# Two equal lists for a routed mixture: the order of row and weight loads changed, and context products moved to the next opening

## What is computed

```python
def _L2_ffn_ref(x, router_logits, gating_einsum, linear, per_expert_scale, router_scale):
...
    var = jnp.mean(jnp.square(x.astype(jnp.float32)), axis=-1, keepdims=True)
    router_input = x * jax.lax.rsqrt(var + 1e-06).astype(dtype)
    root_size = jax.lax.rsqrt(jnp.array(F, dtype=dtype))
    router_input = router_input * root_size * router_scale.astype(dtype)
    logits = jnp.einsum('gsd,de->gse', router_input, router_logits.astype(dtype))
    logits32 = logits.astype(jnp.float32)
    probs = jax.nn.softmax(logits32, axis=-1)
    _, choices = jax.lax.approx_max_k(logits32, k=k)
    indicator = jax.nn.one_hot(choices, E, dtype=probs.dtype).sum(axis=-2)
    renorm = jnp.sum(indicator * probs, axis=-1, keepdims=True)
    renorm = jnp.where(renorm > 0.0, renorm, 1.0)
    weights = probs / renorm
    x_flat = x.reshape((-1, F))
    batch_size = G * S
    choices_flat = choices.ravel()
    xs_order = choices_flat.argsort()
    xs_reverse_argsort = xs_order.argsort()
    xs_indices = jnp.repeat(jnp.arange(batch_size), k)[xs_order]
    sorted_xs = x_flat[xs_indices, :]
    choices_oh = jax.nn.one_hot(choices, num_classes=E, dtype=jnp.int32)
    tokens_per_expert = jnp.sum(choices_oh, axis=(0, 1, 2))
    combine_weights = (choices_oh.astype(jnp.float32) * jnp.expand_dims(weights, axis=2)).sum(axis=-1).astype(weights.dtype)
    w_gate = jnp.transpose(gating_einsum, (0, 3, 1, 2)).reshape(E, F, 2 * H)
    gate_out = jax.lax.ragged_dot(sorted_xs, w_gate.astype(dtype), group_sizes=tokens_per_expert)
    gate_out = gate_out.reshape(gate_out.shape[0], 2, H)
    activation = jax.nn.gelu(gate_out[:, 0, :]) * gate_out[:, 1, :]
    expert_outputs = jax.lax.ragged_dot(activation, linear.astype(dtype), group_sizes=tokens_per_expert)
    expert_indices = jnp.repeat(jnp.arange(E), tokens_per_expert, total_repeat_length=expert_outputs.shape[0])
    expert_outputs = expert_outputs * per_expert_scale.astype(expert_outputs.dtype)[expert_indices, None]
    out = expert_outputs[xs_reverse_argsort].reshape((G, S, k, -1))
    out = jnp.einsum('blkd,blk->bld', out, combine_weights, preferred_element_type=out.dtype)
    return out
```

```python
    kvx = jnp.einsum('bsi,oi->bso', cond, w_kv_x)
    kx, vx = jnp.split(kvx, 2, axis=-1)
    kx = _ln(kx.reshape(b, sc, g, d), kxln_w, kxln_b)
    vx = vx.reshape(b, sc, g, d)
    xout = _gqa(qx, kx, vx).reshape(b, s, nh * d)
```

## Time and profile before

| | us |
|---|---|
| median of three runs | 1403.51 |
| lowest, highest | 1401.1, 1404.28 |
| profiled execution | 1401.32 |
| its span, first to last instruction | 1399.6 |

### The profile page before, as it was taken

The page is one execution under the profiler, slowest core; times in us unless marked ns, Lnnn a source line. Parts: engine busy times, 40 slices in busy tenths (PEclk is TensorE's granted clock), DMA queues, the critical chain, the costliest instruction groups (busy, mean ns, idle before and its releaser), DMA issues.

```text
span 1399.6 us, 23540 instructions
## 1 busy us (share of the span) xinstructions
PE 1272.7 (91%) x7122; PEld 1067.1 (76%) x7122; DVE 965.6 (69%) x2457; ACT 814.7 (58%) x2055; POOL 671.1 (48%) x720
## 2 busy tenths in 40 slices
PE   6999999997899999978559789999999999999994
PEld 3556888885688888868558478888887788888884
DVE  7997556766877777543226577878777787877753
ACT  6954222334666766634224486677777778776353
POOL 1112555542444444442124266666768767675444
PEclk9999999999999999989779999999999999999997
DMA  6224555452212232245234693000240001024283
GB/s 237 83 91 134 171 168 165 114 175 80 101 62 91 81 99 94 101 167 186 90 126 144 230 335 120 1 2 1 64 140 31 31 32 61 31 59 162 85 302 115
DMA packets 90140, 159.62 MB, mean 114 GB/s; under 512 B 9325, under 2 KB 50953, under 8 KB 89516
## 3 DMA queue, kind: packets, MB, share of 16 engines
q1 hardware_dynamic: 82811, 144.55, 31.4%
q0 software_dynamic: 6640, 12.67, 2.7%
q10 hardware_dynamic: 576, 1.05, 0.2%
HBM read 103.86 MB, written 58.17 MB: 116 GB/s over the span
## 4 chain that ended last, share of the span: by engine, by line
PE 69%; DVE 12%; issue 6%; ACT 4%; DMA 4%; POOL 4%; SPq 0%; ACTq 0%; POOLq 0%; DVEq 0%
PE ps L1609 9%; PE ps L1741 9%; PE ps L1714 8%; PE ps L1692 7%; PE ps L1759 7%; PE ps L1623 5%; PE ps L1881 5%; PE ps L1724 5%; PE ps L1703 3%; PE ps L1442 3%; DMA mid_x<-mid_rows 2%; POOL urs L1147 2%; PE ps L1892 2%; DVE usum L3242 1%; PE ps L2046 1%
## 5 line engine op out<-in xcount | busy, mean ns | idle before, releaser
L1154 POOL TENSOR_TENSOR probs<-probs,prec 128x512 f32<-128x512 f32 x192 | 202.7, 1056 | 280.5 <-DVE prec L3278 280.5
L2463 ACT ACTIVATE probs<-ps,nmax 128x256 f32<-128x256 f32 x384 | 179.3, 474 | 184.8 <-DVE nmax L3271 119.0
L1714 PE MATMUL ps<-k_feat,q_feat 128*128 128x256 f32 x768 | 198.6, 381 | 2.7 <-ACT q_feat L2453 1.9
L1741 PE MATMUL ps<-probs_t,v_tok 128*128 128x256 f32 x768 | 197.7, 380 | 0.2 <-ACT ob L2482 0.2
L1147 POOL TENSOR_TENSOR urs<-uve,neg_half 128x4 f32<-128x4 f32 x136 | 137.2, 1009 | 52.2 <-DVE uve L3243 41.5
L1714 PEld LDWEIGHTS ps<-k_feat,q_feat 128*128 128x128 f32 x768 | 136.7, 191 | 16.6 <-issue 3.5
L1741 PEld LDWEIGHTS ps<-probs_t,v_tok 128*128 128x128 f32 x768 | 130.9, 190 | 10.4 <-issue 0.6
L1724 PE MATMUL ps<-ident,probs 128*128 128x128 f32 x768 | 116.4, 274 | 14.9 <-ACT probs_t L2472 13.4
L1724 PEld LDWEIGHTS ps<-ident,probs 128*128 128x128 f32 x768 | 92.4, 141 | 48.0 <-issue 20.9
L2472 ACT ACTIVATE probs_t<-ps 128x512 f32<-128x512 f32 x192 | 115.8, 603 | 2.7 <-PE ps L1724 2.7
L2382 ACT ACTIVATE gated<-ps 128x512 f32<-128x512 f32 x48 | 28.8, 599 | 135.5 <-PE ps L1609 135.5
(11 more groups left out here) (489 smaller groups left out, 3437.1 us busy)
## 6 DMA issues: line engine op xcount, KB each, us to landing
rows_in<-zero_rows SPq DMA_DIRECT2D x3, 5200.0 KB, 33.9
mid_more_w<-in_l2f_w SPq DMA_DIRECT2D x14, 768.0 KB, 4.3
tile_w<-in_l3f_w SPq DMA_DIRECT2D x21, 385.5 KB, 6.7
mid_rows<-mid_zero SPq DMA_DIRECT2D x6, 1040.0 KB, 5.6
w<-in_l1f_w SPq DMA_DIRECT2D x24, 256.0 KB, 4.9
spread_w<-we_dram SPq DMA_DIRECT2D x16, 384.0 KB, 3.7
mid_w<-in_l2f_w SPq DMA_DIRECT2D x8, 768.0 KB, 5.9
kv_cross<-kv_out SPq DMA_DIRECT2D x20, 256.0 KB, 2.0
```

The lines of the kernel that those rows point to most:

```text
L1154: pool.tensor_tensor(p3, p3, spread(prec[g % 3][:, :], [P, TB, S]), ALU.mult)\
L1714: mm = pe.matmul(ps[g % 2][:, j * S:(j + 1) * S], q_feat[:, h, j * P:(j + 1) * P], k_feat[:, kv, :], start=True, stop=True)
L1741: mm = pe.matmul(ps[6][:, 0:S], v_tok[:, tb, kv * P:(kv + 1) * P], probs_t[g % 2][:, tb, :], start=tb == 0, stop=tb == TB - 1)
L2463: ins = act_e.activation(probs[g % 4][:, j, :], ps[g % 2][:, j * S:(j + 1) * S], ACT.Exp, bias=nmax[g % 3][:, j:j + 1], **kw, accum_out=ps ...
```

## The change

Two lists of two batches each take the place of lists of three and one. Both have 8 fixed and 7 later tiles: list A is tiles 0 to 14, list B tiles 15 to 29. Only batches 0 and 1 are routed ahead of the loop; batches 2 and 3 are routed inside it, each with steps of its own. SP's order is written anew: rows are issued in runs, and the weight sets behind them. The three context products ahead of the first tile move into the opening of the next attention, and all eight late products are stored behind the loads of `mid_got` and of `wo` (the next attention's output weights). The next norm of batch 2 moves from the end of the loop into the opening, and the turns of batches 0 and 1 to loop turns 26 and 27.

```diff
-KV_LATE_AT = ((-6, -4, -3), (-7, -5, -4))
+KV_LATE_AT = ((-6, -4, -3), (-6, -5, -5, -4, -4, -3))
...
-MID_TILES = ((0, 19), (19, 30))
-MID_LATER = (11, 3)
-MID_BLOCKS = (6, 2)
-MID_BASE = (0, 6 * MID + 1)
-MID_LISTS = 6 * MID + 1 + 2 * MID + 1
+MID_TILES = ((0, 15), (15, 30))
+MID_LATER = (7, 7)
+MID_BLOCKS = (4, 4)
+MID_BASE = (0, 4 * MID + 1)
+MID_LISTS = 2 * (4 * MID + 1)
...
-KV_WITH_MID = 3
...
-                sp.wait_ge(*mid_at("placed", 16 * CHOICES * 3 * TB))
+                half = NT // 2
+                sp.wait_ge(*mid_at("placed", 16 * CHOICES * half))
+                sp.wait_ge(s["o_ready"], L2X.total)
                 for j in range(MID_RING):
                     rows(j)
                 experts_of, blocks = registers(0)
                 sp.wait_ge(s["out_ready"], L2X.total)
                 for i in range(MID_SETS):
                     later(i)
-                store_kv(len(KV_ALL) - KV_GAPS[2], len(KV_ALL) - KV_GAPS[2] + KV_WITH_MID, kv_late)
                 first_b = MID_TILES[1][0]
                 for j in range(MID_RING, first_b):
                     rows(j)
-                    i = j - MID_RING - 3 + MID_SETS
-                    if MID_SETS <= i < MID_LATER[0]:
-                        later(i)
+                later(MID_SETS)
+                later(MID_SETS + 1)
                 sp.wait_ge(*mid_at("placed", 16 * CHOICES * NT))
-                for j in range(first_b, first_b + MID):
+                for j in range(first_b, first_b + 4):
                     rows(j)
+                later(MID_SETS + 2)
+                rows(first_b + 4)
                 more = registers(1)
                 experts_of, blocks = experts_of + more[0], blocks + more[1]
-                for i in range(MID_LATER[0], sum(MID_LATER)):
+                for i in range(4):
+                    later(MID_SETS + 3 + i)
+                    rows(first_b + 5 + i)
+                for j in range(first_b + 9, MID_ALL - 3):
+                    rows(j)
+                for i in range(4):
+                    sp.wait_ge(*mid_put_all(first_b, i))
+                for b in range(2):
+                    load_mid_got(b)
+                for j in range(MID_ALL - 3, MID_ALL):
+                    rows(j)
+                for i in range(sum(MID_LATER) - 3, sum(MID_LATER)):
                     later(i)
                 for i in range(4):
-                    sp.wait_ge(*mid_put_all(first_b, i))
-                kv_all_stored(len(KV_ALL) - KV_GAPS[2] + KV_WITH_MID)
-                for b in range(3):
+                    sp.wait_ge(*mid_put_all(MID_ALL, i))
+                for b in range(2, B):
                     load_mid_got(b)
-                for j in range(first_b + MID, MID_ALL):
-                    rows(j)
-                store_kv(len(KV_ALL) - KV_GAPS[2] + KV_WITH_MID, len(KV_ALL) - 3, kv_late)
-                for i in range(4):
-                    sp.wait_ge(*mid_put_all(MID_ALL, i))
-                load_mid_got(3)
...
-            store_kv(len(KV_ALL) - 3, len(KV_ALL), kv_late)
+            store_kv(len(KV_ALL) - KV_GAPS[2], len(KV_ALL), kv_late)
...
-                if t == 65:
+                if t == 63:
                     pool.wait_ge(*mid_at("zeroed", 16 * MID_ZERO_AT))
                     pool.wait_ge(*mid_at("places", 1))
-                if 65 <= t < 69:
+                if 63 <= t < 67:
                     mid_scatter(2)
 
             run(attention(L2X, beside_l2x))
-            pool.wait_ge(*mid_at("places", 2))
-            mid_scatter(4)
             part_scales(1)
             root_mean_square(2)
             for j in range(MID_ALL):
                 pool.indirect_dma_start(mid_out[:, :], bass.IndirectOffsetOnAxis(ap=mid_to[:, j:j + 1], axis=0),
                                         mid_y[j % 4][:, :], None, bounds_check=CHOICES * NTOK - 1,
                                         oob_is_err=False).then_inc(mid_signal(f"put{j % 4}"), 16)
-                if j == 11:
-                    pool.wait_ge(*mid_at("places", 4))
-                if 11 <= j < 15:
-                    mid_scatter(1)
-                if j in (22, 23, 24):
+                if j in (4, 7):
+                    pool.wait_ge(*mid_at("places", 3 + (j - 4) // 3))
+                if j in (4, 5, 7, 8):
+                    mid_scatter(2)
+                if j in (20, 21):
...
-                if t in (57, 58, 60):
-                    b = (57, 58, 60).index(t)
-                    if b == 0:
-                        pe.wait_ge(at["l2x"]["raw_ready"], len(L2X.normed))
-                    turn_part(SECOND_LN, b, h_mid, quantised, (SECOND_LN - 1) * B + b + 1, ps[2 + b % 2])
-                if t == 60:
+                if t == 57:
+                    pe.wait_ge(at["l2x"]["raw_ready"], len(L2X.normed))
+                    for b in range(2):
+                        turn_part(SECOND_LN, b, h_mid, quantised, (SECOND_LN - 1) * B + b + 1, ps[2 + b])
+                if t == 59:
+                    mid_logits(0)
+                if t == 61:
                     pe.wait_ge(at["l2x"]["turn_out"], len(L2X.normed))
-                    mid_logits(0)
-                if t == 62:
-                    mid_logits(1)
-                if t == 63:
                     mid_ranks(0)
-                if t == 66:
-                    mid_ranks(1)
 
             run(attention(L2X, toward_mid))
 
...
                 mm.then_inc(mid_signal("down"), 1)
 
             pe.wait_ge(at["l2x"]["exp_ready"], L2X.total)
-            keys_values(KV_WITH_MID, ps[0:2])
-            pe.wait_ge(kv_copied, kv_done[0])
             pe.wait_ge(at["l2x"]["o_out"], L2X.total)
             mid_turn(0)
             for j in range(MID_ALL + 2):
...
                     mid_gates(j)
                 if j == 2:
                     pe.wait_ge(at["l2x"]["y_added"], B)
-                if j == 4:
+                if j == 0:
+                    turn_part(SECOND_LN, 2, h_mid, quantised, SECOND_LN * B - 1, ps[4])
+                if j == 3:
                     turn_part(SECOND_LN, 3, h_mid, quantised, SECOND_LN * B, ps[4])
-                if j == 6:
-                    mid_logits(2)
-                if j == 10:
-                    mid_ranks(2)
-                if j >= MID_ALL - 1:
-                    b = j - MID_ALL + 1
-                    turn_part(LAST_LN, b, h_late, quantised, (LAST_LN - 1) * B + b + 1, ps[4 + b % 2])
+                if j in (2, 5):
+                    mid_logits(1 + (j - 2) // 3)
+                if j in (5, 8):
+                    mid_ranks(1 + (j - 5) // 3)
+                if j in (26, 27):
+                    b = j - 26
+                    turn_part(LAST_LN, b, h_late, quantised, (LAST_LN - 1) * B + b + 1, ps[4 + b])
...
-            act_e.wait_ge(parked, 32 * PARKS)
-            keys_values(KV_WITH_MID, ps[0:2], kv_late)
...
-                if 12 <= j < 20:
-                    high_self(j - 12)
-                if MID_ALL - 2 <= j < MID_ALL + 1:
-                    centre_part(LAST_LN, j - MID_ALL + 2, h_late)
-                if MID_ALL + 1 <= j:
-                    copy_late(LAST_LN, j - MID_ALL - 1)
-            copy_late(LAST_LN, 2)
+                if j in (5, 8):
+                    mid_exp(1 + (j - 5) // 3)
+                if 11 <= j < 19:
+                    high_self(j - 11)
+                if j in (25, 26):
+                    centre_part(LAST_LN, j - 25, h_late)
+                if j in (28, 29):
+                    copy_late(LAST_LN, j - 28)
+            act_e.wait_ge(parked, 32 * PARKS)
...
-                if j == 8:
-                    mid_best_two(2)
+                if j in (3, 6):
+                    part = 1 + (j - 3) // 3
+                    if part == 2:
+                        mid_places(1)
+                    mid_best_two(part)
+                    mid_masks(part)
+                if j in (5, 8):
+                    mid_marked(1 + (j - 5) // 3)
                 if j == 9:
-                    mid_masks(2)
+                    mid_places(2)
                 if j == 10:
-                    mid_marked(2)
-                if j == 11:
-                    mid_places(2)
-                if j == 12:
                     mid_map(1)
-                if 13 <= j < 21:
-                    low_self(j - 13)
-                if j in (24, 25, 26):
-                    mid_add(j - 24)
-                    part_moments(LAST_LN, j - 24)
-                if j in (26, 27, 28):
-                    part_shift(LAST_LN, j - 26)
+                if 12 <= j < 20:
+                    low_self(j - 12)
+                if j in (21, 22):
+                    mid_add(j - 21)
+                    part_moments(LAST_LN, j - 21)
+                if j in (23, 24):
+                    part_shift(LAST_LN, j - 23)
...
-                if t == 0:
-                    mid_add(3)
-                    part_moments(LAST_LN, 3)
-                if t == 3:
-                    part_shift(LAST_LN, 3)
+                if t in (0, 1):
```

(61 more changed lines are left out.)

18 lines of the change are left out of this document (9 added, 9 removed).

## The result

The changed kernel takes 1366.5 us (median of four runs, 1365.5 to 1368.3) against 1402.4 (the three runs shown above and the profiled one): a ratio of 0.9744, interval 0.9727 to 0.9762. It is faster, by 36 us; the forecast was 47, with 1355. The time lies in the range, near its upper end, where the second rival stood (1363). The profiled execution took 1367.0 us with a span of 1365.2, 34.4 less than before.

A forecast was written before the change was run, and what follows sets the result against it. PE, busy 91%, was held up by seven circles of product, row load and turn. Terms −49.5 − 9.9 + 2.0 + 7 + 2.6 − 3.0 + 4 = −46.8 from 1401.3 gave 1354.5, stated as 1355; range 1345 to 1368.

The forecast's parts named there:

- the second rival: Opening of the last attention: stores land as the buses allow, copies 5 to 8 each hold ACT; loss 12, 1363; chance 0.18.
- Seven circles: Routed mixture, seven tiles: rows queued behind weights that wait for `mid_down`; issuing rows ahead gains 49.5 us.
- the routing: Mixture loop: batch 2's turn, logits and ranks now take PE time there; loss 2.0 us, DVE's share costed at nothing.
- the middle: Tiles 12 and 14: weights land late, then one restart at the low clock; loss 7 us, bounds 0 and 12.
- the last three tiles: Loop's end: their weights wait for `mid_down` of tiles 23, 24 and 25; loss 2.6 us.
- the tail: From the last gates to the context products: two norm turns move into the loop, the third into the opening; gain 3.0 us.
- The start: First mixture tile: fewer scatters ahead of it and slots worked out earlier; gain 9.9 us, bounds 5.1 and 12.
- DVE in the loop: Mixture loop: DVE's added routing work fits its idle time and `mid_down`'s slack; cost nothing, 4 us without that cover.
- The opening: Last attention's opening: moved products and norm, eight copies sharing four buffers, stores behind loads; loss 4 us, bounds 0 and 12.
- The late list: List 2's 15 tiles: rows arrive only just in time, each 7.1 us over the pace; 1460 us; chance 0.03.

The follow-up runs named there:

- the second execution: The changed kernel itself, unaltered, measured once more on the same chip as two combined kernels: 1364.2 us (0.9732).
- The last move on DVE: Changed kernel with four stores ahead of `wo` and both `mid_add` moved, batch 3's add now at opening step 3 instead of step 2: 1356.2 us (0.9654).

## Why the prediction was right, and where not

- *Seven circles.* Right. With the routing, the middle, the last three tiles and the tail, the loop was forecast 40.9 us shorter and is 39.25 (38.0 in the second execution); its last product ended at 721.7 (719). Tile 12 waited 1.87 (1.5 forecast), tile 14 3.69 and 1.4 more of gates at the low clock, granted 0.57 there (3.9 and 1.1): the last scatter of list B ended 8.8 us after turn 10 began and the weights landed at 17.7 (9.3 and 17). Tiles 27 and 29 waited 2.59 together (2.6). The last gates stand 5.2 us ahead of the context products, where they stood 8.3: 3.1 (3.0).
- *The start.* 8.7 of 9.9. The last scatter ends at 612.09, 9.6 us earlier than before; its landing and the rows' took 4.65 us instead of 3.7.
- *DVE in the loop* hid its routing, as costed at nothing: none of PE's waits in the loop is ended by DVE.
- *The opening* is the step that failed in size: loss 4 forecast, with bounds 0 and 12; 11.0 measured to the fourth query copy (9.3 in the second execution), 11.8 by the middle of that attention. The rest to the span's 34.4 lies in the last layer, where the second execution was another 4 us shorter, so it can't be laid to the change.
- Inside this term two readings were wrong. I took the first buffer to be free near 12.4 us after the loop, adding landings as if each transfer's median held in a queue of six; it was 18.0. The 3.7 us of the earlier trace rows, held against the second rival, hide a warning: of those five stores two stood ahead of `wo`, and the slowest of the three behind it took 8.0:

```profile
DMA to landing us min/median/max: 2.0/3.7/8.0
```

- The second rival, by which the stores land behind the bytes of `wo` and `mid_got`, held: the first store landed at 740.2, 0.65 us behind the last `wo` load (739.55). Its 15 was still too early (18.0 measured), and ACT waited once for long, 8.38 us, not at each of the copies 5 to 8. The bytes alone don't explain it: with the first four stores issued by ACT the third landed 0.53 and 2.07 us ahead of two `wo` loads issued before it (739.15, 739.68, 741.22).
- And I hid `mid_add` behind 3.09 us of DVE's idle time. That idle time comes after the step's chain, for PE; `mid_add` stands ahead of the chain's next sums, so it shifted all that follows, 3.0 us at like clocks. The last move on DVE gave 3.2 back at the high clock (20.05 to 16.84); the 4.5 from 21.35 to 16.84 has PE's clock in it too. In the kernel before an add stood at step 0 already, batch 3's; that it cost anything isn't shown, as that order took 17.06 at the high clock, hardly more than the last move.
- *The late list*, the rival on the other side, didn't come: no turn of tiles 15 to 29 waits for rows.

Not settled: how far the wait of the fifth copy and the three products share their cost, since each of the two undone alone gives back nearly the same 7 us (6.8 and 7.2 of 8.0); and what of the wait is the queue, the sharing and the late issue, as only the third and fourth stores tell queue from sharing.

## What to carry to other kernels

A load that could go must not stand behind a weight load that waits for a product: one such edit of the queue's order gave 33 us here, the whole new plan 36. When loads or stores are grouped behind others on a queue, work out the landing of the first one that somebody waits for from all bytes ahead of it (here the first store landed 10.9 us after its issue, behind six loads of 512 KB), and look who holds its buffer. Look whether the idle time that is to cover added work lies between that work and the next instruction of the chain: the 3.09 us of idle time just behind the chain hid nothing of the 2.6 us added here, and the stretch grew by 3.0.

## What was not expected of the hardware

A store of 256 KB landed in 2.0 us when ACT issued it 1.3 us ahead of six loads, in 10.9 when SP issued it behind them, and in 6.5 and 7.1 when ACT issued it behind the first loads of `wo`, whose own landing went from 7.7 to 9.4 us. And profiled executions of one kernel differed by 5.6 us in span (1365.2 and 1359.6): 1.8 was there by the fourth query copy, most of it in a stretch whose granted clock was 0.76 and 0.94, and some 4 came behind the last attention, 2.3 ahead of the last layer's tile loop and the rest in it.
